# Mixture-of-experts stage of a fused Perceiver kernel: fp32 products replaced by three float32r products of split factors, and work begun one stage earlier

## The chip, the cores and the metric

One core of one Trainium2 chip runs the whole program. The metric is the device time of one execution in microseconds (us); the median of three runs is compared.

## What is computed

Two layers of a Perceiver block on x of shape (2, 256, 256), that is 512 tokens in four tiles of 128 (NT = 4), with a context of 2 x 4096 tokens. Layer 0: cross-attention with 16 heads, low-rank self-attention with 8 heads, and a mixture of 16 experts. Layer 1: cross-attention with top-k and film modulation, retention, and a mixture of adapters. The stage that matters here is the mixture of layer 0, all in fp32:

```
n      = layernorm(x)                       # 512 x 256
probs  = softmax(n @ gate_w.T)              # 16 experts, four kept and rescaled
for e in range(16):                         # every expert is computed for every token
    h  = silu(n @ w1[e]) * (n @ w3[e])      # 512 x 128
    y += weight[:, e] * (h @ w2[e])         # 512 x 256
x      = x + y
```

Between them stands a product of weights alone, the *film products* `Wv @ W_film` (192 x 256 by 256 x 512, twice), which layer 1 reads later.

## The kernel before

The program is written engine by engine, with semaphores (`Flag`): `flag.up(instruction)` counts up when an instruction ends, `engine.wait_ge(*flag.at(n))` waits for a count. Each engine runs its instructions in the order in which they are written; no scheduler moves them. The program is a row of stages. At the end of each, `phase_ends` puts a barrier over all engines, so that a stage begins when the slowest engine is through with the one before. `bank` is the accumulation memory, eight banks of 128 x 512.

**The keys stage**, at the start, already works with split factors: `ch`, `cl` and `w1h`, `w1l` are the high and the low part of a number in float32r, high being the rounded number and low the rest. Its matmuls are L524 (512 columns) and L531 (256 columns).

**The low-rank stage** (`low_*`, L957 to L1131) goes over the four token tiles: `scores(i)` (L1016), the maxima on VectorE (L1101), the exponentials on ScalarE (L1071), `turn` (L1027, transposes), a copy on VectorE (L1109), `weigh` (L1036) and `divide`. Its sync program also fetches `wv1`, `wv2` and `film`. POOL has two small instructions in it.

**The mixture stage** (`moe_*`, L1154 to L1300). TensorE turns `wv1` and `wv2`, then the normalised tokens (L199), then the gate weights (L1179), and makes the gate scores (L1185). VectorE makes the routing weights from them (L1253 to L1274). Then comes a loop over experts. `up(e)` is the pair of products with w1 and w3: four matmuls of 512 columns (L1206) into two banks; two pairs of banks alternate. ScalarE takes Silu of one bank (L1241), VectorE multiplies it with the other (`times_gate`, L1282) into `hid`. `down(e)` is the product with w2: four matmuls of 256 columns (L1217), again with two pairs of banks in turn; VectorE adds them to x with the routing weight (`add`, L1290). TensorE's order is one up ahead:

```
pe.wait_ge(*nm_made.at(1))
up(0)
film_products()
for e in range(NE):
    if e + 1 < NE:
        up(e + 1)
    down(e)
```

Weights lie in four buffers; the sync engine refills one when its down is done. After the stage's barrier the preparation of layer 1 follows (L1373 and on).

## Time and profile before

| | |
|---|---|
| median of 3 runs | 1168.22 us (1164.32 to 1171.87) |
| profiled execution | 1164.9 us, its span 1163.7 us |
| TensorE busy | 969.7 us (83%), 7503 matmuls |
| VectorE, ScalarE busy | 829.5 us (71%), 627.7 us (54%) |
| POOL busy | 258.4 us (22%) |
| granted TensorE clock, mean | 0.889 of 2.4 GHz |
| low-rank stage | about 535 to 594 us of the span |
| mixture stage | about 594 to 702 us of the span |

PE is TensorE's matmul, PEld its weight load, DVE VectorE, ACT ScalarE, SPq the sync engine's DMA queue. A share of busy time is a mean over stages; in the mixture stage TensorE is busy without a break from 606.5 us on, while in the low-rank stage no engine is.

### The profile page before, as it was taken

The numbers are of one execution on the slowest core, as the hardware profiler recorded it, in microseconds if no ns is written. First come the engines' busy times: TensorE is split into PE (matmuls) and PEld (weight loads), VectorE is DVE, ScalarE is ACT, GpSimd is POOL, SyncE is SP. The second block draws the span as 40 slices with busy tenths as digits, with TensorE's granted clock in tenths as the row PEclk, the third lists the DMA queues.
The fourth block names the chain that finished last, engine by engine and source line by source line (L and its number), as shares of the span: only waits on it lengthen the run. The fifth ranks groups of instructions, "written<-read, shape, count | busy, mean of one in ns | idle before, by whom it ended". The sixth has DMA issues, their size and how long they took to land. (4 is left out here: it accounts for less than half of the span.)

```text
span 1163.7 us, 20413 instructions
## 1 busy us (share of the span) xinstructions
PE 969.7 (83%) x7503; PEld 589.6 (51%) x7520; DVE 829.5 (71%) x1753; ACT 627.7 (54%) x1018; POOL 258.4 (22%) x281
## 2 busy tenths in 40 slices
PE   6997769999999999985879998518878878996586
PEld 5886624444444444443765565314455555744354
DVE  5775688999999999913542447998888786256447
ACT  3443317887887888872331114139999998202121
POOL 1000188899300000000000002003554632000010
PEclk9999959999999999997769998558799998997797
DMA  5867632223223223102011216302164226740000
GB/s 179 312 226 256 254 113 73 74 79 83 73 77 86 73 75 86 44 1 57 1 55 62 85 44 181 96 0 60 38 173 133 69 80 213 176 137 1 0 1 19
DMA packets 99319, 111.80 MB, mean 96 GB/s; under 512 B 26658, under 2 KB 75730, under 8 KB 99218
## 3 DMA queue, kind: packets, MB, share of 16 engines
q1 hardware_dynamic: 96802, 109.50, 31.2%
q10 hardware_dynamic: 2416, 0.99, 0.4%
q8 instruction: 60, 0.98, 0.3%
q14 instruction: 41, 0.34, 0.1%
HBM read 80.95 MB, written 29.43 MB: 95 GB/s over the span
## 5 line engine op out<-in xcount | busy, mean ns | idle before, releaser
L835 ACT ACTIVATE pT<-bank 128x512 f32<-128x512 f32 x512 | 278.4, 597 | 93.5 <-PE bank L752 72.2
L857 DVE TENSOR_REDUCE rmax<-bank 128x2 f32<-128x1024 f32 x256 | 307.3, 1223 | 26.5 <-PE bank L720 25.7
L764 PE MATMUL bank<-pT,V 128*17 128x256 f32 x2048 | 161.1, 387 | 4.7 <-ACT oT L841 4.6
L1600 PE MATMUL bank<-K1s,qs 97*128 97x512 f32 x256 | 116.1, 555 | 58.6 <-ACT below L1709 37.2
L752 PEld LDWEIGHTS bank<-qs,ks 49*128 49x128 f32 x1024 | 77.8, 187 | 112.4 <-ACT pT L835 98.9
L752 PE MATMUL bank<-qs,ks 49*128 49x256 f32 x1024 | 130.0, 332 | 2.3 <-ACT pT L835 0.5
L1864 POOL TENSOR_TENSOR total<-total,work 128x1024 f32<-128x1024 f32 x40 | 94.9, 2380 | 154.7 <-ACT work L1718 153.9
L720 PE MATMUL bank<-ks,qs 49*128 49x512 f32 x512 | 110.6, 427 | 16.4 <-DMA ks<-k_parts_d 9.2
L1600 PEld LDWEIGHTS bank<-K1s,qs 97*128 97x128 f32 x256 | 54.0, 224 | 73.9 <-ACT below L1709 38.6
L1770 DVE MAX8 cand<-work 128x8 f32<-128x128 f32 x384 | 76.5, 280 | 0.0
L764 PEld LDWEIGHTS bank<-pT,V 128*17 128x17 f32 x2048 | 34.6, 95 | 63.0 <-ACT pT L835 43.6
L720 PEld LDWEIGHTS bank<-ks,qs 49*128 49x128 f32 x512 | 51.5, 196 | 26.3 <-issue 13.9
L1206 PE MATMUL bank<-xT,w 128*128 128x512 f32 x128 | 60.6, 619 | 0.6 <-DVE nm L1254 0.6
L1634 PE MATMUL bank<-cn,xT 128*128 128x192 f32 x256 | 55.9, 368 | 6.2 <-ACT xT L1728 6.2
L1718 ACT ACTIVATE work<-bank,ebias 128x1024 f32<-128x1024 f32 x48 | 54.9, 1149 | 5.7 <-PE bank L1603 5.4
L1687 ACT COPY work<-bank 128x1024 f32<-128x1024 f32 x48 | 50.8, 1058 | 5.9 <-PE bank L1600 5.9
L1634 PEld LDWEIGHTS bank<-cn,xT 128*128 128x128 f32 x256 | 46.8, 213 | 11.2 <-ACT xT L1728 10.4
L974 POOL MEMSET vA<- 128x32 f32 x1 | 0.2, 154 | 232.4 <-POOLq L113 232.4
L1709 ACT ACTIVATE below<-work,steep_thr 128x2048 bf16<-128x2048 f32 (+1 forms) x26 | 50.2, 1932 | 1.2 <-issue 0.6
L1603 PE MATMUL bank<-below,minus 128*128 128x512 bf16 x111 | 48.2, 434 | 0.0
L1241 ACT ACTIVATE gate<-bank 128x512 f32<-128x512 f32 x16 | 9.6, 597 | 71.0 <-PE bank L1206 71.0
L1282 DVE TENSOR_TENSOR hid<-bank,gate 128x512 f32<-128x512 f32 x16 | 11.1, 692 | 46.2 <-ACT gate L1241 46.2
...
## 6 DMA issues: line engine op xcount, KB each, us to landing
k_parts_d<-kparts SPq DMA_DIRECT2D x48, 512.0 KB, 3.6
...
```

The costliest lines, as they stand in the source:

```text
L720: t = pe.matmul(bank[:, 2 * (at % 2) + a, :], qs[p % 3][rows, qt * P:(qt + 1) * P], ks[p % 2][rows, c * 512:(c + 1) * 512], start=True, st ...
L752: t = pe.matmul(bank[:, 4 + (at + a) % 3, c * S:(c + 1) * S], ks[p % 2][rows, k0:k0 + P], qs[p % 3][rows, :], start=True, stop=True)
L764: t = pe.matmul(bank[32 * c:32 * c + VW, 7, a * S:(a + 1) * S], V[:, b * NCH + 4 * g + c, h, :], pT[:, (at + 2 * (c // 2) + a) % 8, c % 2 ...
L835: p_made.up(act.activation(pT[:, at % 8, :], bank[:, 4 + at % 3, :], ACT.Exp))
L857: max_read.up(dve.tensor_reduce(rmax[p % 2][:, :, qt, c], bank[:, b0:b0 + 2, :], AX.X, ALU.max))
L1206: t = pe.matmul(bank[:, 2 * j + k, :], w13[e % 4][:, k, kt, :], xT[:, kt, :], start=(kt == 0), stop=(kt == 1))
L1600: m = pe.matmul(bank[:, b0 + c, :], qs1[0:NROW1, b * H1 + h, q], K1s[h][0:NROW1, keys], start=True, stop=(what == "new"))
L1634: m = pe.matmul(bank[:, 7, grp % 2 * 256:grp % 2 * 256 + DC], aT[at % 2][:, c, :], cn[at % NCN][:, c, :], start=(n == 0 and c == 0), stop= ...
L1687: s_taken.up(act.copy(home(t)[:, k * 1024:(k + 1) * 1024], bank[:, b0:b0 + 2, :].rearrange("p c n -> p (c n)")))
L1718: s_taken.up(act.activation(home(t)[:, k * 1024:(k + 1) * 1024], bank[:, b0:b0 + 2, :].rearrange("p c n -> p (c n)"), ACT.Exp, bias=ebias[ ...
L1770: m = dve.max(cand[:, g, :], home(t)[:, g * GC:(g + 1) * GC])
L1864: added.up(pool.tensor_tensor(acc[:, part], acc[:, part], home(t)[:, part], ALU.add))
```

## The change

1. In the mixture stage every fp32 factor is split in a high and a low part of type float32r, and a product is the sum of three: high by high, low of the one by high of the other, and the reverse (`PRODUCTS`). The low-by-low product is left out. The split of the tokens (`xTp`) is made once; that of each expert's weights by `expert_high` (ScalarE, rounding copy) and `expert_low` (POOL, subtraction); that of `hid` by `high` (ScalarE) and `low` (VectorE).
2. The ups use three pairs of banks in turn (0 to 5), and run two experts ahead; the downs have one pair (6, 7), and wait bank by bank for the additions of the expert before.
3. The weights of experts 0 to 3 are fetched and split in the low-rank stage. So are `gwr` and `wv` turned there, and the first half of the film products (128 of 192 rows) is made there behind `scores(0)`; the second half (64 rows) is the first work of the mixture stage. VectorE copies the first half, ScalarE the second.
4. `up(0)` waits for the split tokens and no longer for the maxima of the gate scores.

```diff
+    NE, FI, TOP, PAD, WB = 16, 128, 4, 4, 4
...
+    w13p = [sb(f"w13p{j}", [P, 2, 2, 2, FI], F32R) for j in range(WB)]
+    w2p = [sb(f"w2p{j}", [P, 2, D], F32R) for j in range(WB)]
...
+    def load_expert(e):
+        for k, w in enumerate((ins["L0_ffn_w1"], ins["L0_ffn_w3"])):
+            w_in[e % WB].up(sp.dma_start(w13[e % WB][:, k, :, :], w[e].rearrange("(k p) i -> p k i", p=P)), 16)
+        w_in[e % WB].up(sp.dma_start(w2e[e % WB][:, :], ins["L0_ffn_w2"][e]), 16)
+
+    def expert_high(e):
+        j = e % WB
+        act.wait_ge(*w_in[j].at(48 * (e // WB + 1)))
+        wh_split.up(act.copy(w13p[j][:, 0, :, :, :], w13[j][:, :, :, :]))
+        wh_split.up(act.copy(w2p[j][:, 0, :], w2e[j][:, :]))
+
+    def expert_low(e):
+        j = e % WB
+        pool.wait_ge(*wh_split.at(2 * e + 1))
+        wl_split.up(pool.tensor_tensor(w13p[j][:, 1, :, :, :], w13[j][:, :, :, :], w13p[j][:, 0, :, :, :], ALU.subtract))
+        pool.wait_ge(*wh_split.at(2 * e + 2))
+        wl_split.up(pool.tensor_tensor(w2p[j][:, 1, :], w2e[j][:, :], w2p[j][:, 0, :], ALU.subtract))
+
+    FILM_ROWS = (slice(0, P), slice(P, DC))
+
+    def film_products(n, first_bank):
+        pe.wait_ge(*film_w_in.at(32))
+        pe.wait_ge(*wvT_made.at(1))
+        rows = FILM_ROWS[n]
+        for k in range(2):
+            for kt in range(2):
+                t = pe.matmul(bank[0:rows.stop - rows.start, first_bank + k, :], wvT[:, kt, rows], film[:, k, kt, :],
+                              start=(kt == 0), stop=(kt == 1))
+            wvf_made.up(t)
...
+        gate_in.up(sp.dma_start(gwr[:, :], ins["L0_ffn_gate_w"]), 16)
         for k, n in enumerate(("in", "out")):
             film_w_in.up(sp.dma_start(film[:, k, :, :], halves("L1_xattn_W_film_" + n)), 16)
+        for e in range(WB):
+            load_expert(e)
...
         mrow_made.up(pool.tensor_scalar(mrow[:, :], m8[:, :], 1e18, -1e18, ALU.mult, ALU.add))
+        for e in range(WB):
+            expert_low(e)
...
+        pe.wait_ge(*wv_in.at(32))
+        pe.wait_ge(*gate_in.at(16))
+        pe.wait_ge(*qk_made[0].at(1))
+        for kt in range(2):
+            pe.transpose(bank[:, 4, kt * DC:kt * DC + P], wv1[:, kt * P:(kt + 1) * P], ident[:, :])
+            pe.transpose(bank[:, 4, kt * DC + P:(kt + 1) * DC], wv2[:, kt * P:(kt + 1) * P], ident[0:DCM, 0:DCM])
+            t = pe.transpose(bank[:, 4, 2 * DC + kt * NE:2 * DC + (kt + 1) * NE], gwr[:, kt * P:(kt + 1) * P], ident[0:NE, 0:NE])
+        wv_turned.up(t)
         pe.wait_ge(*vA_made.at(NT))
         scores(0)
-        for i in range(NT):
+        film_products(0, 6)
+        for i in range(NT):
+            if i == 0:
+                pe.wait_ge(*wvT_made.at(2))
             turn(2 * i)
+            if i == 0:
+                pe.wait_ge(*wvf_copied.at(2))
             turn(2 * i + 1)
...
+        act.wait_ge(*wv_turned.at(1))
+        wvT_made.up(act.copy(wvT[:, :, :].rearrange("p k c -> p (k c)"), bank[:, 4, 0:2 * DC]))
+        wvT_made.up(act.copy(gwT[:, :, :].rearrange("p a b -> p (a b)"), bank[:, 4, 2 * DC:2 * DC + 2 * NE]))
...
+            expert_high(i)
...
         maxima(0)
+        for k in range(2):
+            dve.wait_ge(*wvf_made.at(k + 1))
+            wvf_copied.up(dve.tensor_copy(wvf1[:, k, :], bank[:, 6 + k, :]))
...
+    xTp = sb("xTp", [P, 2, 2, T], F32R)
...
+    hidp = [sb(f"hidp{j}", [P, 2, T], F32R) for j in range(3)]
+
+    PRODUCTS = ((0, 0), (1, 0), (0, 1))
...
-        for e in range(NE):
-            if e >= 4:
-                sp.wait_ge(*y_made.at(e - 3))
-            for k, w in enumerate((ins["L0_ffn_w1"], ins["L0_ffn_w3"])):
-                w_in[e % 4].up(sp.dma_start(w13[e % 4][:, k, :, :], w[e].rearrange("(k p) i -> p k i", p=P)), 16)
-            w_in[e % 4].up(sp.dma_start(w2e[e % 4][:, :], ins["L0_ffn_w2"][e]), 16)
+        for e in range(WB, NE):
+            sp.wait_ge(*wl_split.at(2 * (e - WB + 1)))
+            sp.wait_ge(*wh_split.at(2 * (e - WB + 1)))
+            load_expert(e)
...
+        film_products(1, 4)
         pe.wait_ge(*ln_made.at(4 * 3))
         turn_tensor(tokens_of(xn))
...
+        def up(e):
+            b0 = 2 * (e % 3)
+            pe.wait_ge(*wh_split.at(2 * e + 1))
+            pe.wait_ge(*wl_split.at(2 * e + 1))
+            if e >= 3:
+                pe.wait_ge(*hid_done.at(e - 2))
+            for k in range(2):
+                for n, (wp, xp) in enumerate(PRODUCTS):
                     for kt in range(2):
-                        t = pe.matmul(bank[0:rows.stop - rows.start, 4 + 2 * n + k, :], wvT[:, kt, rows], film[:, k, kt, :],
-                                      start=(kt == 0), stop=(kt == 1))
-                    wvf_made.up(t)
-
-        def up(e):
-            j = e % 2
-            pe.wait_ge(*w_in[e % 4].at(48 * (e // 4 + 1)))
-            if e >= 2:
-                pe.wait_ge(*hid_done.at(e - 1))
-            for k in range(2):
-                for kt in range(2):
-                    t = pe.matmul(bank[:, 2 * j + k, :], w13[e % 4][:, k, kt, :], xT[:, kt, :], start=(kt == 0), stop=(kt == 1))
+                        t = pe.matmul(bank[:, b0 + k, :], w13p[e % WB][:, wp, k, kt, :], xTp[:, xp, kt, :],
+                                      start=(n == 0 and kt == 0), stop=(n == 2 and kt == 1))
             gu_made.up(t)
 
         def down(e):
-            j = e % 2
-            pe.wait_ge(*hid_done.at(e + 1))
-            if e < 2:
-                pe.wait_ge(*wvf_copied.at(2 * e + 2))
-            else:
-                pe.wait_ge(*y_added.at(NT * (e - 1)))
+            pe.wait_ge(*wh_split.at(2 * e + 2))
+            pe.wait_ge(*wl_split.at(2 * e + 2))
+            pe.wait_ge(*hh_split.at(e + 1))
+            pe.wait_ge(*hl_split.at(e + 1))
             for i in range(NT):
-                t = pe.matmul(bank[:, 4 + 2 * j + i // 2, (i % 2) * D:(i % 2 + 1) * D], hid[j][:, i * P:(i + 1) * P],
-                              w2e[e % 4][:, :], start=True, stop=True)
-            y_made.up(t)
-
+                if i % 2 == 0 and e:
+                    pe.wait_ge(*y_added.at(NT * (e - 1) + i + 2))
+                for n, (hp, wp) in enumerate(PRODUCTS):
+                    t = pe.matmul(bank[:, 6 + i // 2, (i % 2) * D:(i % 2 + 1) * D], hidp[e % 3][:, hp, i * P:(i + 1) * P],
+                                  w2p[e % WB][:, wp, :], start=(n == 0), stop=(n == 2))
+                if i % 2:
+                    y_made.up(t)
+
+        pe.wait_ge(*xh_split.at(2))
+        pe.wait_ge(*xl_split.at(2))
+        up(0)
+        up(1)
+        pe.wait_ge(*wvf_copied.at(4))
         pe.wait_ge(*nm_made.at(1))
-        up(0)
-        film_products()
         for e in range(NE):
-            if e + 1 < NE:
-                up(e + 1)
+            if e + 2 < NE:
+                up(e + 2)
...
+    def moe_pool():
+        for e in range(WB, NE):
+            expert_low(e)
...
+        for k in range(2):
+            act.wait_ge(*wvf_made.at(3 + k))
+            wvf_copied.up(act.copy(wvf2[:, k, :], bank[0:DCM, 4 + k, :]))
+        for kt in range(2):
+            act.wait_ge(*turned.at(2 * 3 + kt + 1))
+            xT_made.up(act.copy(xT[:, kt, :], bank[:, kt, :]))
+            xh_split.up(act.copy(xTp[:, 0, kt, :], bank[:, kt, :]))
...
-        for e in range(NE):
+
+        def silu(e):
             act.wait_ge(*gu_made.at(e + 1))
             if e >= 2:
                 act.wait_ge(*hid_done.at(e - 1))
-            gate_done.up(act.activation(gate[e % 2][:, :], bank[:, 2 * (e % 2), :], ACT.Silu))
-            if e == 0:
-                for n, (dst, rows) in enumerate(((wvf1, P), (wvf2, DCM))):
-                    for k in range(2):
-                        act.wait_ge(*wvf_made.at(2 * n + k + 1))
-                        wvf_copied.up(act.copy(dst[:, k, :], bank[0:rows, 4 + 2 * n + k, :]))
+            gate_done.up(act.activation(gate[e % 2][:, :], bank[:, 2 * (e % 3), :], ACT.Silu))
+
+        def high(e):
+            act.wait_ge(*hid_done.at(e + 1))
+            if e >= 3:
+                act.wait_ge(*y_made.at(2 * (e - 2)))
+            hh_split.up(act.copy(hidp[e % 3][:, 0, :], hid[e % 2][:, :]))
+
+        for e in range(NE + 2):
+            if e < NE:
+                silu(e)
+                high(e)
+            if e >= 2 and e - 2 + WB < NE:
+                act.wait_ge(*gu_made.at(e - 1))
+                act.wait_ge(*y_made.at(2 * (e - 1)))
+                expert_high(e - 2 + WB)
...
+        for kt in range(2):
+            dve.wait_ge(*xh_split.at(kt + 1))
+            xl_split.up(dve.tensor_tensor(xTp[:, 1, kt, :], bank[:, kt, :], xTp[:, 0, kt, :], ALU.subtract))
...
         def times_gate(e):
-            j = e % 2
             dve.wait_ge(*gate_done.at(e + 1))
             if e >= 2:
-                dve.wait_ge(*y_made.at(e - 1))
-            hid_done.up(dve.tensor_tensor(hid[j][:, :], bank[:, 2 * j + 1, :], gate[j][:, :], ALU.mult))
+                dve.wait_ge(*hh_split.at(e - 1))
+            hid_done.up(dve.tensor_tensor(hid[e % 2][:, :], bank[:, 2 * (e % 3) + 1, :], gate[e % 2][:, :], ALU.mult))
+
+        def low(e):
+            dve.wait_ge(*hh_split.at(e + 1))
+            hl_split.up(dve.tensor_tensor(hidp[e % 3][:, 1, :], hid[e % 2][:, :], hidp[e % 3][:, 0, :], ALU.subtract))
 
         def add(e):
-            j = e % 2
-            dve.wait_ge(*y_made.at(e + 1))
             if e:
                 dve.wait_ge(*y_added.at(NT * e))
             for i in range(NT):
-                y_added.up(dve.scalar_tensor_tensor(x[:, i, :], bank[:, 4 + 2 * j + i // 2, (i % 2) * D:(i % 2 + 1) * D],
+                if i % 2 == 0:
+                    dve.wait_ge(*y_made.at(2 * e + i // 2 + 1))
+                y_added.up(dve.scalar_tensor_tensor(x[:, i, :], bank[:, 6 + i // 2, (i % 2) * D:(i % 2 + 1) * D],
                                                     weight[:, i, e:e + 1], x[:, i, :], ALU.mult, ALU.add))
 
-        times_gate(0)
+        for e in range(2):
+            times_gate(e)
+            low(e)
         for e in range(NE):
-            if e + 1 < NE:
-                times_gate(e + 1)
+            if e + 2 < NE:
+                times_gate(e + 2)
             add(e)
+            if e + 2 < NE:
+                low(e + 2)
```

In the low-rank stage, TensorE's order changes as follows (`wv` and `gwr` are the weights that are turned, `sA` the exponentials). Before:

```order
L1004 MATMUL bank<-lowW,xT 128x32 x32
L1016 MATMUL bank<-low_k,low_q 128x256 x8
L1027 MATMUL bank<-ident,sA 128x128 x16
L1016 MATMUL bank<-low_k,low_q 128x256 x8
```

And in the changed kernel:

```order
L1052 MATMUL bank<-lowW,xT 128x32 x32
L1092 MATMUL bank<-ident,wv_8517 128x128
L1093 MATMUL bank<-ident,wv_8518 128x64
L1094 MATMUL bank<-ident,gwr 128x16
L1092 MATMUL bank<-ident,wv_8517 128x128
L1093 MATMUL bank<-ident,wv_8518 128x64
L1094 MATMUL bank<-ident,gwr 128x16
L1064 MATMUL bank<-low_k,low_q 128x256 x8
L977 MATMUL bank<-film,wvT 128x512 x4
L1075 MATMUL bank<-ident,sA 128x128 x16
```

Six transposes stand ahead of scores(0), and four film matmuls between it and the first turn.

On TensorE from the start of the mixture stage (the numbers in the names count buffers). Before:

```order
L199 MATMUL bank<-ident,xn 128x128 x8
L1179 MATMUL bank<-ident,gwr 128x16 x2
L1185 MATMUL bank<-gwT,xT 128x16 x8
L1206 MATMUL bank<-xT,w_0_9036 128x512 x4
L1195 MATMUL bank<-film,wvT 128x512 x4
L1195 MATMUL bank<-film,wvT 64x512 x4
L1206 MATMUL bank<-xT,w_1_9037 128x512 x4
L1217 MATMUL bank<-w2e_9040,hid_9055 128x256 x4
```

And in the changed kernel:

```order
L977 MATMUL bank<-film,wvT 64x512 x4
L199 MATMUL bank<-ident,xn 128x128 x8
L1239 MATMUL bank<-gwT,xT 128x16 x8
L1252 MATMUL bank<-xTp,w13p_8531 128x512 x12
L1252 MATMUL bank<-xTp,w13p_8532 128x512 x12
L1252 MATMUL bank<-xTp,w13p_8533 128x512 x12
L1265 MATMUL bank<-w2p_8535,hidp_9131 128x256 x12
L1252 MATMUL bank<-xTp,w13p_8534 128x512 x12
L1265 MATMUL bank<-w2p_8536,hidp_9132 128x256 x12
```

Three ups stand ahead of the first down where there were two, each of twelve matmuls instead of four. At the other end two downs stand without an up between them, where there were two before as well.

## Rows read from the trace of the kernel before

**Rows 1.** Page, costliest groups: count, then busy us and mean ns, then idle before

```profile
L1206 PE MATMUL bank<-xT,w 128*128 128x512 f32 x128 | 60.6, 619 | 0.6 <-DVE nm L1254 0.6
L1241 ACT ACTIVATE gate<-bank 128x512 f32<-128x512 f32 x16 | 9.6, 597 | 71.0 <-PE bank L1206 71.0
L1282 DVE TENSOR_TENSOR hid<-bank,gate 128x512 f32<-128x512 f32 x16 | 11.1, 692 | 46.2 <-ACT gate L1241 46.2
```

**Rows 2.** Timeline of the mixture stage, in pieces: start us, length us, engine, line

```profile
606.54 6.56 PE L1206 MATMUL bank<-xT,w 128*128 128x512 f32 x8 [0.57 <-DVE nm L1254]
...
612.93 1.45 PE L1195 MATMUL bank<-film,wvT 128*128 128x512 f32 x3
...
620.03 3.70 PE L1206 MATMUL bank<-xT,w 128*128 128x512 f32 x8
...
692.38 3.60 PE L1206 MATMUL bank<-xT,w 128*128 128x512 f32 x8
...
695.81 3.62 PE L1217 MATMUL bank<-w2e,hid 128*128 128x256 f32 x16
...
697.74 3.42 DVE L1290 SCALAR_TENSOR_TENSOR x<-bank,weight,x 128x256 f32<-128x256 f32 x8 [0.41 <-PE bank L1217]
```

**Rows 3.** Windows: length, busy us of PE, PEld, DVE, ACT, POOL, clock, DMA

```profile
594.40:606.50 12.10, 7.30 (x30) 6.06 (x30) 4.15 (x17) 4.42 (x6) 0.00 (x0) 0.50 0.45 131
606.50:613.00 6.50, 6.46 (x9) 2.78 (x10) 3.04 (x32) 2.56 (x9) 0.00 (x0) 0.55 0.00 0
...
620.00:640.00 20.00, 20.00 (x62) 11.61 (x62) 7.17 (x16) 2.97 (x5) 0.00 (x0) 1.00 0.28 90
```

**Rows 4.** Timeline of the keys stage, one block's float32r matmuls, first and last

```profile
60.11 0.39 PE L524 MATMUL bank<-ch,w1h 128*128 128x512 f32 x1
...
62.17 0.40 PE L524 MATMUL bank<-c,w2l 128*128 128x512 f32 x1
62.41 0.28 PE L531 MATMUL bank<-w1h,ch 128*128 128x256 f32 x1
...
64.58 0.28 PE L531 MATMUL bank<-w2l,c 128*128 128x256 f32 x1
```

**Rows 5.** Windows, the same stretch of the keys stage

```profile
60.00:64.80 4.80, 4.80 (x32) 4.20 (x30) 3.94 (x6) 2.18 (x4) 0.00 (x0) 1.00 0.41 155
```

**Rows 6.** Groups kept apart by shape, VectorE and POOL: busy us, mean ns

```profile
L443 DVE TENSOR_TENSOR qparts<-qf,qparts 128x512 fp32r<-128x512 f32 x2 | 1.4, 692 | 0.1
...
L1864 POOL TENSOR_TENSOR total<-total,work 128x1024 f32<-128x1024 f32 x40 | 94.9, 2380 | 154.7 <-ACT work L1718 153.9
...
L602 POOL TENSOR_TENSOR fr<-g,g 128x128 f32<-128x128 f32 x9 | 4.1, 456 | 0.7
```

**Rows 7.** Timeline of the low-rank stage up to the first copy of turned scores

```profile
541.91 0.47 SPq L969 DMA_DIRECT2D film<-in_L_xattn_W_film_out  x1
...
552.85 1.15 PE L1016 MATMUL bank<-low_k,low_q 32*128 32x256 f32 x16 [1.87 <-DVE vA L1093]
...
556.39 3.03 ACT L1071 ACTIVATE sA<-bank,mA 128x256 f32<-128x256 f32 x8 [5.26 <-DVE mA L1101]
...
558.01 3.46 PE L1027 MATMUL bank<-ident,sA 128*128 128x128 f32 x16 [4.01 <-ACT sA L1071]
...
560.02 1.23 DVE L1109 COPY sAT<-bank 128x1024 f32<-128x1024 f32 x1 [3.66 <-PE bank L1027]
```

**Rows 8.** DMA issues: count, KB each, median us from issue to landing

```profile
film<-in_L_xattn_W_film_out SPq DMA_DIRECT2D x1, 512.0 KB, 7.1
```

**Rows 9.** Timeline of the seam before the first up

```profile
599.66 1.97 PE L199 MATMUL bank<-ident,xn 128*128 128x128 f32 x8 [3.71 <-DVE xn L184]
...
602.40 3.57 PE L1185 MATMUL bank<-gwT,xT 128*128 128x16 f32 x16 [0.45 <-ACT xT L205]
...
610.54 0.65 DVE L1274 TENSOR_SCALAR weight<-weight,den 128x16 f32<-128x16 f32 x4
```

More of the change, by code:

```diff
@@ L932, in build @@
     wvf_d = nc.dram_tensor("wvf_d", [DC, 2, 2 * D], F32).ap()
+    NE, FI, TOP, PAD, WB = 16, 128, 4, 4, 4
+    w13 = [sb(f"w13_{i}", [P, 2, 2, FI]) for i in range(WB)]
+    w2e = [sb(f"w2e_{i}", [P, D]) for i in range(WB)]
+    w13p = [sb(f"w13p{j}", [P, 2, 2, 2, FI], F32R) for j in range(WB)]
+    w2p = [sb(f"w2p{j}", [P, 2, D], F32R) for j in range(WB)]
+    gwr = sb("gwr", [NE, D])
+    gwT = sb("gwT", [P, 2, NE])
+    w_in = [flag(f"w_in{i}") for i in range(WB)]
+    gate_in, wh_split, wl_split = flag("gate_in"), flag("wh_split"), flag("wl_split")
@@ L933, in build @@
     mask_d = nc.dram_tensor("mask_d", [NB, S2], F32).ap()
     mask_in, mrow_made, mask_stored = flag("mask_in"), flag("mrow_made"), flag("mask_stored")
-    film_w_in, wv_turned, wvT_made, wvf_made, wvf_copied, wvf_stored = (flag(n) for n in (
-        "film_w_in", "wv_turned", "wvT_made", "wvf_made", "wvf_copied", "wvf_stored"))
+    wv_in, film_w_in, wv_turned, wvT_made, wvf_made, wvf_copied, wvf_stored = (flag(n) for n in (
+        "wv_in", "film_w_in", "wv_turned", "wvT_made", "wvf_made", "wvf_copied", "wvf_stored"))
@@ L1132, in build @@
     phase_ends()
-    NE, FI, TOP, PAD = 16, 128, 4, 4
     phase_begins()
-    w13 = [sb(f"w13_{i}", [P, 2, 2, FI]) for i in range(4)]
-    w2e = [sb(f"w2e_{i}", [P, D]) for i in range(4)]
-    gwr = sb("gwr", [NE, D])
-    gwT = sb("gwT", [P, 2, NE])
     lg = sb("lg", [P, NT, NE])
@@ L1169, in moe_tensor @@
     def moe_tensor():
-        pe.wait_ge(*film_w_in.at(64))
-        for kt in range(2):
-            pe.transpose(bank[:, 4, kt * DC:kt * DC + P], wv1[:, kt * P:(kt + 1) * P], ident[:, :])
-            t = pe.transpose(bank[:, 4, kt * DC + P:(kt + 1) * DC], wv2[:, kt * P:(kt + 1) * P], ident[0:DCM, 0:DCM])
-        wv_turned.up(t)
+        film_products(1, 4)
         pe.wait_ge(*ln_made.at(4 * 3))
         turn_tensor(tokens_of(xn))
-        pe.wait_ge(*gate_in.at(16))
-        for kt in range(2):
-            t = pe.transpose(bank[:, 2, kt * NE:(kt + 1) * NE], gwr[:, kt * P:(kt + 1) * P], ident[0:NE, 0:NE])
-        gw_turned.up(t)
-        pe.wait_ge(*gwT_made.at(1))
         pe.wait_ge(*xT_made.at(8))
@@ L1184, in moe_tensor @@
             for kt in range(2):
-                t = pe.matmul(bank[:, 3, i * NE:(i + 1) * NE], xT[:, kt, i * P:(i + 1) * P], gwT[:, kt, :],
+                t = pe.matmul(bank[:, 7, i * NE:(i + 1) * NE], xT[:, kt, i * P:(i + 1) * P], gwT[:, kt, :],
                               start=(kt == 0), stop=(kt == 1))
         lg_made.up(t)
-        def film_products():
-            pe.wait_ge(*wvT_made.at(1))
-            for rows, n in ((slice(0, P), 0), (slice(P, DC), 1)):
-                for k in range(2):
-                    for kt in range(2):
-                        t = pe.matmul(bank[0:rows.stop - rows.start, 4 + 2 * n + k, :], wvT[:, kt, rows], film[:, k, kt, :],
-                                      start=(kt == 0), stop=(kt == 1))
-                    wvf_made.up(t)
@@ L1231, in moe_scalar @@
-        wvT_made.up(act.copy(wvT[:, :, :].rearrange("p k c -> p (k c)"), bank[:, 4, 0:2 * DC]))
         norm_scalar(2)
-        turn_scalar(3)
+        for k in range(2):
[5 more added lines that the diff above has]
+            xh_split.up(act.copy(xTp[:, 0, kt, :], bank[:, kt, :]))
```

21 lines of the change are left out of this document (7 added, 14 removed).

## The prediction, made before the changed kernel ran

> **What bounds the kernel now.** I read the page first (which engines are busy in which stretch), then the costliest groups, then the mixture stage in order of time, then the two neighbours that receive moved work. The chain of waits at the end of the page covers only the last few per cent of the span, so it says nothing on this stage; who waits for whom there must be read from the groups and the timeline.
>
> In the mixture stage TensorE never waits: its first products (L1206) sat idle 0.6 us in all before 128 instructions, while ScalarE waited 71.0 us for them and VectorE 46.2 us for ScalarE [rows 1]. The timeline shows the period. The first up(0) starts at 606.54; the film products start at 612.93; up(1) at 620.03, and up(15) at 692.38, so 14 pairs of one up and one down take 72.35 us, **5.17 us a pair** [rows 2]. Then come up(15) (3.43), two downs (3.62) and VectorE's last additions until 701.16. Adding up: 6.39 + 7.10 + 72.35 + 3.43 + 3.62 + 1.73 = **94.6 us** from 606.54 to 701.16. The windows say at what clock: 0.50 in the part before 606.5, 0.55 until 613, 1.00 after it, with TensorE busy 20.00 of 20.00 us [rows 3]. So up(0) paid 6.39 us for the work that later costs 3.43.
>
> **The price of a split product.** The kernel already multiplies float32r factors in its keys stage, in both forms that the change uses: 128 weights by 512 columns (L524) and by 256 columns (L531). Starts are to be compared there, not durations, since matmuls overlap. From 60.11 to 62.17 lie 9 starts: 0.229 us each; from 62.41 to 64.58 lie 19: 0.114 us each [rows 4], at a granted clock of 1.00 [rows 5]. An fp32 matmul is two instructions in the trace (x8 for four in the program), a float32r one is one. Hence an up becomes 12 x 0.229 = 2.75 us (was 3.43), a down 12 x 0.114 = 1.37 us (was 1.73): **4.12 us a pair**, three products included. The nearest other row is the fp32 matmul itself, 3.43 / 4 = 0.857 us, four times 0.214 [rows 2]. If a float32r matmul were exactly a quarter of it, the pair would cost 3.9; I take 4.12 because rows 4 are the very form.
>
> The Trainium skill (TensorE: Matmul & The Clock Gate, "Back-to-back issue gap") gives N / 2.4 + 2.5 ns warm, 216 ns for 512 columns and 109 ns for 256. By it the pair would be 3.90 us and the stage some 4 us shorter still; the rows of the keys stage do not agree with it, being 6% above.
>
> **Does another engine become the bound?** Per expert, VectorE has its product with the gate (0.69), a new subtraction (0.69, as L443 [rows 6]) and four additions (3.42 / 8 = 0.43 each [rows 2], 1.71): 3.1 of 4.12 us. ScalarE has Silu of 512 elements (0.60 [rows 1]) and three casts of 512 or fewer, taken at the same price: at most 2.4. POOL has two subtractions of 512 and 256 elements; between 0.456 us for 128 and 2.38 for 1024 [rows 6] lies a line that gives 1.28 + 0.73 = 2.0. The waits fit too. Counted from the end of up(e+2): Silu, gate product and additions of e are done after about 3.2 us, and down(e+1), which needs the one pair of result banks, comes after 4.1. ScalarE's cast of hid ends at 2.2, its cast of the next weights at 2.8, POOL's subtraction at 4.1, and up(e+4), which reads them, starts at 1.37 + 2.75 + 1.37 = 5.5. So 0.9 and 1.4 us are left, and TensorE stays the bound. The next weights are asked for four pairs ahead, 16 us, so their transfers stay hidden.
>
> **The sum for the stage.** up(0) to up(15) is 16 x 2.75 = 44.0, down(0) to down(13) beside them 14 x 1.37 = 19.2. Then the single pair of result banks shows: down(14) and down(15) must wait, bank by bank, for the additions before them. VectorE does add(13) 1.7, the last subtraction 0.7, add(14) 1.7, then down(15)'s second half 0.7 + 0.2, then the last two additions 0.9, with hand-overs of some 0.2: 6.1 us (before: downs 3.62 and additions 1.73 after the last up, for two downs). Together 44.0 + 19.2 + 6.1 = **69.3 us against 94.6: 25.3 less**. Some 7.1 of it are the film products, which leave this stretch; 16 instructions, eight to each side.
>
> **Film products, first half, and the transposes, in the low-rank stage.** The six transposes fall between the value products and scores(0), which waits until 552.85 for VectorE, 1.9 us of idle TensorE: hidden. The four matmuls follow scores(0), end of it at 554.0, and the next TensorE work is turn(0) at 558.01 [rows 7]. At the high clock they need 7.10 / 2 = 3.55 us [rows 2]: done at 557.6, before turn(0). At the low clock they need 8 x 0.80 = 6.4 (up(0), rows 2): done at 560.4, 2.4 us late. TensorE was at work shortly before and now does not idle, so I take zero and keep +2.4; on the other side, turn(0) and turn(1) may run at the higher clock, at most 1.5 us of 3.46. The last film weights are issued at 541.91 [rows 7] and take 7.1 us to land [rows 8]: there at 549, or 549.5 behind one more small issue, in time. The two VectorE copies (0.6 to 0.7 each, half of the 1.23 for 1024 elements) stand between the maxima (end 556.4) and the first copy of turned scores at 560.02 [rows 7]: hidden; with the film products late they would end with them, inside the same 2.4 us. The casts of experts 0 to 3 take about 1 us after each tile's exponentials, where ScalarE waits for the next tile's maxima (5.3 us before the first [rows 7]), and POOL had nothing. Twelve DMA issues move ahead of the mask's store on SP's queue; only the next stage needs that store.
>
> **Film products, second half, at the seam.** They need 3.6 us at the high and 6.4 at the low clock from 594.5, in place of 1.4 us of transposes. xn comes at 599.66 as before [rows 9]. At the low clock the turn starts at 600.9, and ScalarE's two copies and then four instead of two transfers of xT (0.59 each) put the gate scores, now at 602.40, up to 2 us later; on the other side TensorE has then worked without a break before the turn, and turn (1.97) and gate scores (3.57 [rows 9]) may run at the high clock. The first up no longer waits for the maxima. I put its start between 604.1 and 607.5 and take **605.5, 1.0 earlier**, and charge half of a low-clock up(0), 1.4 us. VectorE's routing ends 5.2 us after the gate scores, as now (606.0 to 611.2 [rows 9]); down(0) comes 8.2 us after them, behind three ups: hidden, which it was not to the same degree when one up stood there.
>
> **Sum:** -25.3 - 1.0 + 1.4 + 0 = -24.9 us. The profiled execution took 1164.9 us, so 1140.0. The median of the runs is 3.3 above it (1168.2); the changed kernel's median should lie at **1142 us**.
>
> **Rivals.**
> 1. *VectorE and POOL get in each other's way.* The new subtraction on VectorE reads two SBUF tiles, and POOL now works in this stage. No row of this kernel shows such a pair overlapping, so I bound it: nothing, or each subtraction waits for one POOL instruction, 3.1 + 1.28 = 4.4 us a pair, +0.28 x 16 = 4.5; at the outermost for both, 5.1, +15. It gives 1147 to 1157. Against it: POOL idles half of each pair, and VectorE 1 us. The Trainium skill (SBUF — State Buffer, "Who interferes with whom") says that a VectorE instruction with two SBUF inputs and a GpSimd instruction that reads SBUF exclude each other for their whole length. No run here shows it yet; by it this rival is real, and the first bound holds. Chance 0.13.
> 2. *The array takes 3.9 us a pair,* a quarter of the fp32 time for each product: 1138. Chance 0.08.
> 3. *POOL is the bound.* No POOL row writes float32r. From twice the price above (2.0 to 4.1) it sets the pace; at 2.6 times the pair is 5.2 us, as before, and only the film products and the early start are gained, some 8 us: 1160, within the noise. Chance 0.04.
> 4. *Slower: the granted clock stays at 1.2 GHz in the mixture.* Each pair would cost 4.12 more; 24.9 / 4.12 = 6, so from the seventh such pair the kernel is slower than before, and with all 16 it ends at 1208. For it: the seam, with TensorE busy 7.30 of 12.10 us, is at 0.50 [rows 3]. Against it: float32r products in the keys stage are at 1.00 [rows 5], and nothing here leaves TensorE idle. Chance 0.03.
>
> The forecast itself has 0.72. The range takes in the lower rate and the better seam below (1168.2 - 25.3 - 2.4 - 1.5 - 4 = 1135, and 3 us of spread), and above the first port bound with the low-clock film products (1142 + 4.5 + 2.4 and spread): 1132 to 1153. A difference under 1% (11.7 us) can't be told from none here: faster 0.93, same 0.04, slower 0.03.
>
> **What the new profile would show.** Starts of consecutive ups 4.1 us apart with TensorE without a gap; float32r matmuls 0.229 us apart; VectorE's new subtraction at 0.69 us (longer: rival 1); POOL's two at 1.28 and 0.73 (longer: rival 3); clock 1.00 from the first or second up on; turn(0) of the low-rank stage still about 3.9 us after scores(0) ends. I am wrong if an up waits for POOL's weights or a down for additions in mid-stage, or if the low-rank stage grows by more than 3 us.

## The result, and the profile after

| | before | after |
|---|---|---|
| median, same chip | 1170.05 us (4 runs) | **1141.89 us** (1139.02 to 1143.56, 4 runs) |
| profiled execution, its span | 1164.9, 1163.7 us | 1140.79, 1139.5 us |
| low-rank stage | 59.3 us | 56.1 us |
| seam, to the first up | 12.0 us | 9.5 us |
| mixture, first up to last addition | 94.6 us | 72.1 us |
| next stage, to its first product with K1s | 14.6 us | 17.9 us |

The ratio is 0.9766, 95% interval 0.9734 to 0.9798: faster, and the forecast of 1142.0 was met. The medians differ by 28.2 us, the two profiled executions by 24.1. In a second comparison both kernels ran again unchanged (runs r1 and r2, below), and their medians differ by 25.5 us.

The costliest groups of the changed kernel in the window 590 to 673 us, the mixture stage; they answer to [rows 1] and, for the new instructions, to [rows 6]. Columns: shapes and count, busy us and mean ns, idle us before them and what ended it.

```profile
L1252 PE MATMUL bank<-xTp,w13p 128*128 128x512 f32 x192 | 48.7, 406 | 0.0
...
L1265 PE MATMUL bank<-w2p,hidp 128*128 128x256 f32 x192 | 25.3, 280 | 1.4 <-DVE x L1365 1.4
...
L1357 DVE TENSOR_TENSOR hidp<-hid,hidp 128x512 fp32r<-128x512 f32 x16 | 22.0, 1377 | 1.4 <-ACT hidp L1308 1.4
L963 POOL TENSOR_TENSOR w13p<-w,w13p 128x512 fp32r<-128x512 f32 x12 | 15.5, 1291 | 45.4 <-ACT w13p L957 45.4
L965 POOL TENSOR_TENSOR w2p<-w2e,w2p 128x256 fp32r<-128x256 f32 x12 | 14.4, 1196 | 0.0
L1353 DVE TENSOR_TENSOR hid<-bank,gate 128x512 f32<-128x512 f32 x16 | 11.1, 693 | 7.9 <-ACT gate L1302 7.8
```

TensorE still waits for nothing: 0.0 us before 192 up products, 1.4 before the down products, all of it in the tail. But two of the new instructions are longer than forecast: VectorE's subtraction took 1377 ns where 690 was expected (1.61 us in the twelve experts in which POOL works beside it, 0.69 in the other four), POOL's second one 1196 where 730 was. The gate product is unchanged at 693.

The timeline has one whole pair (start us, length us, engine, line, and the idle time before where there was any), then the last up and the tail. It answers to [rows 2].

```profile
600.38 4.13 PE L1252 MATMUL bank<-xTp,w13p 128*128 128x512 f32 x11
...
610.41 1.57 PE L1265 MATMUL bank<-w2p,hidp 128*128 128x256 f32 x12
...
611.82 2.97 PE L1252 MATMUL bank<-xTp,w13p 128*128 128x512 f32 x12
...
616.04 2.97 PE L1252 MATMUL bank<-xTp,w13p 128*128 128x512 f32 x12
616.07 1.65 DVE L1365 SCALAR_TENSOR_TENSOR x<-bank,weight,x 128x256 f32<-128x256 f32 x4
616.18 0.62 ACT L1308 CAST hidp<-hid 128x512 fp32r<-128x512 f32 x1 [0.76 <-DVE hid L1353]
...
616.71 0.62 ACT L957 CAST w13p<-w 128x512 fp32r<-128x512 f32 x1
...
617.40 1.29 POOL L963 TENSOR_TENSOR w13p<-w,w13p 128x512 fp32r<-128x512 f32 x1 [1.76 <-ACT w13p L957]
617.63 1.60 DVE L1357 TENSOR_TENSOR hidp<-hid,hidp 128x512 fp32r<-128x512 f32 x1
...
618.65 1.19 POOL L965 TENSOR_TENSOR w2p<-w2e,w2p 128x256 fp32r<-128x256 f32 x1
...
662.38 2.96 PE L1252 MATMUL bank<-xTp,w13p 128*128 128x512 f32 x12
...
667.64 1.67 PE L1265 MATMUL bank<-w2p,hidp 128*128 128x256 f32 x12 [0.88 <-DVE x L1365]
...
669.80 1.67 PE L1265 MATMUL bank<-w2p,hidp 128*128 128x256 f32 x12 [0.50 <-DVE x L1365]
...
670.86 1.66 DVE L1365 SCALAR_TENSOR_TENSOR x<-bank,weight,x 128x256 f32<-128x256 f32 x4 [0.42 <-PE bank L1265]
```

From up(3) at 611.82 to up(15) at 662.38 lie 12 pairs: **4.213 us each**, where 5.17 stood and 4.12 was forecast. An up takes 2.81 us from its start to that of the down (12 starts, 0.234 each), a down 1.41 (0.1175 each). VectorE's subtraction begins 0.23 us after POOL's and ends at 619.23, 0.54 after POOL's end at 618.69: it does its own work when POOL is through. POOL's second one in turn ends at 619.84, 0.61 after VectorE. The only waits of TensorE are in the tail, for the additions.

Windows of the same trace (length, busy us of PE, PEld, DVE, ACT, POOL, granted clock, DMA), answering to [rows 3]:

```profile
602.00:604.00 2.00, 2.00 (x6) 1.51 (x6) 1.36 (x18) 1.64 (x4) 0.00 (x0) 0.50 0.00 1
604.00:606.00 2.00, 2.00 (x9) 1.58 (x8) 1.90 (x16) 0.60 (x1) 0.00 (x0) 0.78 0.00 0
...
620.00:640.00 20.00, 20.00 (x113) 17.26 (x112) 18.28 (x30) 9.64 (x19) 11.30 (x10) 1.00 0.34 100
```

The clock is at its low level for a part of the first ups, and at the high one from then on, as before. VectorE is now busy 18.28 of 20 us; some of that is standing still behind POOL.

### The profile page after: what moved, and what is told of

Its sections match the earlier page's. It is cut to its first block and busy times, and to the rows that moved or that the text cites. A ratio compares the mean times of both kernels' runs of the same rounds, so it can differ in the third digit from the quotient of the medians.

```text
span 1139.5 us, 20829 instructions
## 1 busy us (share of the span) xinstructions
PE 955.4 (84%) x7631; PEld 599.1 (53%) x7648; DVE 848.7 (74%) x1772; ACT 651.4 (57%) x1067; POOL 295.7 (26%) x313
## 5 line engine op out<-in xcount | busy, mean ns | idle before, releaser
L1713 PE MATMUL bank<-cn,xT 128*128 128x192 f32 x256 | 59.1, 383 | 6.3 <-ACT xT L1807 6.2
L1713 PEld LDWEIGHTS bank<-cn,xT 128*128 128x128 f32 x256 | 49.4, 222 | 11.5 <-ACT xT L1807 10.5
L1252 PE MATMUL bank<-xTp,w13p 128*128 128x512 f32 x192 | 48.7, 406 | 0.0
L963 POOL TENSOR_TENSOR w13p<-w,w13p 128x512 fp32r<-128x512 f32 x16 | 20.6, 1286 | 80.8 <-ACT w13p L957 80.8
L1252 PEld LDWEIGHTS bank<-xTp,w13p 128*128 128x128 f32 x192 | 36.2, 194 | 7.9
```

What stands on the lines that cost most here:

```text
L1252: t = pe.matmul(bank[:, b0 + k, :], w13p[e % WB][:, wp, k, kt, :], xTp[:, xp, kt, :], start=(n == 0 and kt == 0), stop=(n == 2 and kt == 1))
L1713: m = pe.matmul(bank[:, 7, grp % 2 * 256:grp % 2 * 256 + DC], aT[at % 2][:, c, :], cn[at % NCN][:, c, :], start=(n == 0 and c == 0), stop= ...
```

## The experiments

Stage lengths are from each kernel's profile. They are sharper than the medians: the mixture took 72.1 us in the changed kernel's two profiles and in e2's, which shares its code there, while the executions of one kernel spread over 4 to 14 us. Against the kernel before, the intervals of e2, e3, e5, e6 and e8 all overlap that of the changed kernel, so their medians alone part none of them from it.

### What the product is worth: e1

```diff
-    w13p = [sb(f"w13p{j}", [P, 2, 2, 2, FI], F32R) for j in range(WB)]
+    w13p = [sb(f"w13p{j}", [P, 2, 2, 2, FI], F32) for j in range(WB)]
...
-    PRODUCTS = ((0, 0), (1, 0), (0, 1))
+    PRODUCTS = ((0, 0),)
```

w2p, xTp and hidp become fp32 too, so that one fp32 product does the work of the three.

> The changed kernel with all its moves (film products, early weights, order two experts ahead, casts and their buffers) but fp32 products: one matmul per factor pair instead of three, and the copies keep fp32. Theory A (the gain of the mixture is the cheaper product): a pair of up and down costs 5.16 us again instead of 4.21, so the stage is 14 x 0.95 = 13 to 15 us longer and the kernel comes to about 1156 us; half of the 28 us of gain stays, from the moved work. Rival (the gain is order and moves, the product's price does not matter): within 3 us of 1142.

Measured: 1156.97 us, ratio 0.9897 (0.9828 to 0.9966). The mixture took 86.7 us, the seam 9.5. Two consecutive ups in the timeline:

```profile
631.02 3.60 PE L1252 MATMUL bank<-xTp,w13p 128*128 128x512 f32 x8
...
636.18 2.31 PE L1252 MATMUL bank<-xTp,w13p 128*128 128x512 f32 x5
```

They start 5.16 us apart, the price of fp32. So of the 22.5 us by which the mixture became shorter, 14.6 (86.7 to 72.1) are the price of the product and 7.9 (94.6 to 86.7) the moves, above all the film products' 7.1 [rows 2]; with the seam's 2.5 the moves are worth 10.4.

### The film products: e2

```diff
         scores(0)
-        film_products(0, 6)
...
     def moe_tensor():
+        film_products(0, 2)
         film_products(1, 4)
```

Their copies go to ScalarE in the mixture stage, and up(1) waits for them.

> The changed kernel with the first half of the film products back in the mixture stage, before the second half, on banks 2 and 3; its copies go to ScalarE. Theory A (behind scores(0) the film matmuls were free, and beyond that kept the granted clock up, which made the low-rank stage 3.2 us shorter): the low-rank stage goes back to 59 us (+3), the seam before the first up grows by the 3.5 to 6.9 us of eight instructions less what waits for the tokens anyway, some +4; about 1149 us. Rival (the low-rank stage's 3.2 us are chance of that execution): the stage stays at 56 us, about 1146.

Measured: 1147.09 us, ratio 0.9780 (0.9699 to 0.9860); one of its four executions took 4566.31 us, which no trace explains, and the other three lie at 1140.66 to 1147.74. The seam grew from 9.5 to 13.3 us, and the film products there are one group:

```profile
595.21 9.10 PE L977 MATMUL bank<-film,wvT 128*128 128x512 f32 x16 [1.48 <-PEq L113]
```

The mixture stayed at 72.1. The early half is thus worth 3.8 us of seam. What failed is the thought that these products, filling TensorE's idle time, keep the clock high and so shorten the low-rank stage: without them it took 55.8 us, as short as with them.

### Does POOL reach the bound, and what does the exclusion cost: e3, e5

e3 doubles each subtraction of POOL from expert 4 on; e5 cuts them to 4 columns (most of the low parts of those weights are left out).

```diff
+        if e >= WB:
+            gps.then(pool.tensor_tensor(w13p[j][:, 1, :, :, :], w13[j][:, :, :, :], w13p[j][:, 0, :, :, :], ALU.subtract))
         wl_split.up(pool.tensor_tensor(w13p[j][:, 1, :, :, :], w13[j][:, :, :, :], w13p[j][:, 0, :, :, :], ALU.subtract))
```

```diff
-        wl_split.up(pool.tensor_tensor(w13p[j][:, 1, :, :, :], w13[j][:, :, :, :], w13p[j][:, 0, :, :, :], ALU.subtract))
+        m = 1 if e >= WB else FI
+        wl_split.up(pool.tensor_tensor(w13p[j][:, 1, :, :, 0:m], w13[j][:, :, :, 0:m], w13p[j][:, 0, :, :, 0:m], ALU.subtract))
```

> The changed kernel with each of POOL's two subtractions done twice for experts 4 to 15. Theory A (VectorE's subtraction of two SBUF tiles and POOL's instructions shut each other out for their whole length): POOL needs 2 x (1.29 + 0.73) = 4.0 us a pair and cannot start while VectorE's 0.69 runs, nor the reverse, so POOL and VectorE together set the pace: pair 4.7 to 5.4 us instead of 4.21, kernel +6 to +14 us. Rival (they share without shutting out; the 1.60 us of VectorE's subtraction is something else): POOL's 4.0 stays below 4.21, pair unchanged, kernel within 1 us of 1142.

> The changed kernel with POOL's subtraction cut to a few columns for experts 4 to 15, so that their low parts are mostly those of experts 0 to 3 (left out on purpose). Theory A (exclusion, but hidden): VectorE's subtraction falls from 1.60 to 0.69 us, the pair stays 4.21 us, kernel within 1 us of 1142. Rival 1 (VectorE's 1.60 us is its own price for float32r output from SBUF): it stays 1.60. Rival 2 (the exclusion does cost time): the pair falls towards 4.12.

e3 measured 1147.61 us, ratio 0.9808 (0.9740 to 0.9876): the mixture took 76.7 us, 4.6 more, at 4.6 us a pair. In its groups POOL idles for 26.0 us in all, and all of it lies before its first instruction in this stage:

```profile
L964 POOL TENSOR_TENSOR w13p<-w,w13p 128x512 fp32r<-128x512 f32 x12 | 20.5, 1708 | 26.0 <-ACT w13p L957 26.0
L965 POOL TENSOR_TENSOR w13p<-w,w13p 128x512 fp32r<-128x512 f32 x12 | 15.9, 1326 | 0.9
L1361 DVE TENSOR_TENSOR hidp<-hid,hidp 128x512 fp32r<-128x512 f32 x14 | 10.5, 752 | 0.0
...
L968 POOL TENSOR_TENSOR w2p<-w2e,w2p 128x256 fp32r<-128x256 f32 x12 | 8.9, 743 | 0.0
L969 POOL TENSOR_TENSOR w2p<-w2e,w2p 128x256 fp32r<-128x256 f32 x12 | 8.9, 742 | 0.9
```

1.71 + 1.33 + 0.74 + 0.74 = 4.52 us of POOL in a pair of 4.6: POOL has become the bound. Here VectorE's subtraction comes first and is short (0.68 to 0.72 us in all but the first such pair, where it took 1.61), and it is POOL's that is long. The timeline of e3:

```profile
630.06 0.68 DVE L1361 TENSOR_TENSOR hidp<-hid,hidp 128x512 fp32r<-128x512 f32 x1
630.15 1.74 POOL L964 TENSOR_TENSOR w13p<-w,w13p 128x512 fp32r<-128x512 f32 x1
```

So it goes both ways.

e5 measured 1143.68 us, ratio 0.9780 (0.9719 to 0.9842), the mixture 72.2 us at 4.21 a pair, no shorter than with whole subtractions. Its timeline shows two POOL instructions of one size beside and clear of VectorE:

```profile
635.87 0.21 POOL L964 TENSOR_TENSOR w13p<-w,w13p 128x4 fp32r<-128x4 f32 x1 [3.25 <-ACT w13p L957]
636.10 0.68 DVE L1359 TENSOR_TENSOR hidp<-hid,hidp 128x512 fp32r<-128x512 f32 x1
636.18 0.66 POOL L967 TENSOR_TENSOR w2p<-w2e,w2p 128x4 fp32r<-128x4 f32 x1
```

Four columns take POOL 0.21 us alone; 0.08 us behind the start of VectorE's subtraction they take 0.66 and end with it or just after. The subtraction itself is back at 0.68. **The two engines exclude each other, and here it costs nothing**, since no up and no down waits for either: in the pair shown above VectorE's subtraction for down(3) ends at 619.23, and down(3) starts at 623.05, one pair after down(2); POOL's for up(5) ends at 618.69, and up(5) starts at 620.25.

### How far ahead the ups run: e6

```diff
         up(0)
-        up(1)
...
-            if e + 2 < NE:
-                up(e + 2)
+            if e + 1 < NE:
+                up(e + 1)
             down(e)
```

VectorE's order is changed to match.

> The changed kernel with ups one expert ahead instead of two, VectorE's order to match. Theory A (exclusion of VectorE and POOL, hidden by the second expert ahead): down(e) now waits for VectorE's subtraction, which ends only after POOL's, pair 4.6 us, stage +7 us, about 1149. Rival (no exclusion matters): VectorE's subtraction is done 3.9 us after the up, just inside the 4.2, pair 4.22, and only the first and last experts cost 2 us more, about 1144.

Measured: 1147.38 us, ratio 0.9803 (0.9746 to 0.9859); the mixture took 77.9 us, 5.8 more. (Its later stages were also 9 us longer in the profiled execution, which I can't explain; the stage length is the better figure.) The timeline shows the wait:

```profile
632.95 2.97 PE L1252 MATMUL bank<-xTp,w13p 128*128 128x512 f32 x12
...
634.44 1.61 DVE L1356 TENSOR_TENSOR hidp<-hid,hidp 128x512 fp32r<-128x512 f32 x1
...
636.31 1.65 PE L1265 MATMUL bank<-w2p,hidp 128*128 128x256 f32 x12 [0.39 <-DVE hidp L1356]
```

TensorE idles until VectorE's subtraction ends at 636.05, and that one stood behind POOL (1.61 us). At 0.69 us it would have ended at 635.13, before the up beside it was through (635.92); so the wait is put down to the exclusion by this sum, and no run has one up ahead without the exclusion. One up between up(e) and down(e) is too little cover; a second one hides both the chain and the exclusion. Pairs alternate between about 4.3 and 4.9 us.

### Another narrow type: e4 and its repeat r3

```diff
-    w13p = [sb(f"w13p{j}", [P, 2, 2, 2, FI], F32R) for j in range(WB)]
+    w13p = [sb(f"w13p{j}", [P, 2, 2, 2, FI], BF16) for j in range(WB)]
```

w2p, xTp and hidp likewise; the three products are kept. How much exactness it costs is not on record.

> The changed kernel with factors split into two bf16 parts instead of two float32r parts; 24 products a pair as before. Theory A (the 0.234 us between starts is a property of 4-byte factors): starts come 0.216 us apart or less, pair 3.9 us, and with the exclusion of VectorE and POOL perhaps 4.0; stage -3 to -5 us, about 1138. Rival (the spacing comes from the weight loads that alternate with the matmuls, whatever the type): 0.234 stays, pair 4.2, about 1142. Its products are less exact than those of float32r.

> The kernel with bf16 parts once more, beside the changed kernel on the same chip. Theory A (matmuls of 2-byte factors start 0.216 us apart against 0.234): mixture 67.4 against 72.1 us, median 4 to 5 us below the changed kernel's. Rival (the earlier 3.6 us between their medians were chance): within 2 us.

Measured: 1138.33 us, ratio 0.9729 (0.9681 to 0.9777); the repeat 1138.16, ratio 0.9734 (0.9697 to 0.9771). The timeline of e4:

```profile
633.07 2.75 PE L1252 MATMUL bank<-xTp,w13p 128*128 128x512 bf16 x12
635.66 1.47 PE L1265 MATMUL bank<-w2p,hidp 128*128 128x256 bf16 x12
636.97 2.75 PE L1252 MATMUL bank<-xTp,w13p 128*128 128x512 bf16 x12
```

and its group of weight loads, at 98 ns each (the changed kernel's same group, for float32r, has 188):

```profile
L1265 PEld LDWEIGHTS bank<-w2p,hidp 128*128 128x128 bf16 x185 | 17.9, 98 | 7.3 <-issue 2.1 <-DVE x L1365 0.2
```

2.59 us for 12 starts is 0.216 each, 1.31 is 0.109: 3.90 us a pair, the second rival's number, but for bf16. Both the matmuls and their weight loads are shorter with bf16, and no run tells which of the two lowers the spacing. The mixture took 67.4 and 65.5 us; the clock under its first ups stood at 0.50 to 0.67 in the one and at 1.00 in the other. It is the best version in median, 4.3 us below r2. The two intervals overlap slightly, and the stage length is what shows it.

### The stages around it: e7, e8, and both kernels again

e7 is the kernel before with four fp32 matmuls of 512 columns behind scores(0), where the change has its film products; e8 is the changed kernel with two such at the end of each of the first three tiles of the low-rank stage. Their results are read by nobody.

```diff
         scores(0)
+        for k in range(2):
+            for kt in range(2):
+                pe.matmul(bank[:, 6 + k, :], ident[:, :], ones[:, :], start=(kt == 0), stop=(kt == 1))
```

```diff
             weigh(2 * i + 1)
+            for k in range(2 if i + 1 < NT else 0):
+                pe.matmul(bank[:, 5, :], ident[:, :], ones[:, :], start=(k == 0), stop=(k == 1))
```

> The kernel before with nothing changed but four fp32 matmuls of 512 columns, whose result nobody reads, behind scores(0), where the changed kernel has its film products. Theory A (filling TensorE there keeps the granted clock up): the low-rank stage falls from 59.3 to about 56 us although work is added, kernel -3 us. Rival (the film products only moved into idle time): the stage stays at 59.3 us, kernel unchanged or slower.

> The changed kernel with two more fp32 matmuls of 512 columns, whose result nobody reads, at the end of each of the first three tiles of the low-rank stage, where TensorE waits for the exponentials. Theory A (idle stretches there let the clock fall, and each tile at the low clock takes 9.8 instead of 7.8 to 8.3 us): tiles 2 and 3 fall to about 8 us, low-rank stage -2 to -3 us, about 1139. Rival (filling one gap does not hold the clock through the small products of the weigh step): tiles as now or the fill is in the way, 1142 to 1144.

> The kernel before, unchanged, profiled once more. Theory A (the low-rank and the preparation stage have several lengths for one and the same program, by where in them the granted clock falls and rises): low-rank stage 59.3 or some 56 us, preparation up to the first scores 14.6 or 17.6 to 19 us. Rival (the low-rank stage is 59.3 us in this program and 56 in the changed one): 59.3 again. Mixture from its first up to its last addition 94.7 us either way.

> The changed kernel, unchanged, profiled once more. Theory A: mixture 72.1 us and seam 9.5 us again, low-rank stage 56.1 or 59.2, preparation 14.6 or 17.9; median about 1142. Rival (the preparation is 3 us longer in the changed kernel): 17.9 again.

| us | run | ratio (interval) | low-rank | seam | mixture | next stage's start |
|---|---|---|---|---|---|---|
| e7 | 1169.46 | 1.0010 (0.9985 to 1.0034) | 59.2 | 12.0 | 94.7 | 17.7 |
| e8 | 1147.31 | 0.9820 (0.9773 to 0.9867) | 58.2 | 10.2 | 70.6 | 14.6 |
| r1, before | 1167.97 | 0.9997 (0.9973 to 1.0022) | 59.4 | 12.0 | 94.7 | 14.6 |
| r2, after | 1142.43 | 0.9786 (0.9745 to 0.9826) | **59.0** | 9.9 | 72.1 | **14.6** |
| after, first profile | 1141.89 | 0.9766 (0.9734 to 0.9798) | **56.1** | 9.5 | 72.1 | **17.9** |

The last two lines are one program. Its low-rank stage lasted 56.1 us in one execution and 59.0 in the other, and the start of the next stage 17.9 and 14.6: both differences are the granted clock's. In the low-rank stage, the first profile of the changed kernel, the windows where the film products L977 run:

```profile
552.80:554.80 2.00, 2.00 (x17) 0.94 (x13) 1.28 (x1) 0.79 (x1) 0.00 (x0) 1.00 0.02 4
554.80:556.80 2.00, 2.00 (x6) 0.74 (x4) 1.61 (x2) 0.95 (x3) 0.00 (x0) 1.00 0.00 0
```

its timeline:

```profile
553.38 3.70 PE L977 MATMUL bank<-film,wvT 128*128 128x512 f32 x8
...
557.56 1.06 PE L1075 MATMUL bank<-ident,sA 128*128 128x128 f32 x8 [0.48 <-ACT sA L1135]
```

and the same windows and timeline of r2:

```profile
553.50:555.50 2.00, 2.00 (x16) 0.88 (x11) 1.28 (x1) 0.79 (x1) 0.00 (x0) 0.72 0.01 1
555.50:557.50 2.00, 2.00 (x4) 0.75 (x3) 1.02 (x1) 0.95 (x3) 0.00 (x0) 0.50 0.00 0
```

```profile
554.09 5.40 PE L977 MATMUL bank<-film,wvT 128*128 128x512 f32 x8
559.32 2.04 PE L1075 MATMUL bank<-ident,sA 128*128 128x128 f32 x16
```

With the clock falling to the low level under them, the film products take 5.40 us instead of 3.70, and turn(0) starts 5.2 us after the end of scores(0) instead of 4.1 (4.0 in the kernel before). At the start of the next stage it is the first execution that has the low level. The clock, in windows, and its 16 projections, in the timeline:

```profile
681.00:683.00 2.00, 1.23 (x5) 0.67 (x4) 0.00 (x0) 1.73 (x3) 0.00 (x0) 0.50 0.71 223
683.00:685.00 2.00, 2.00 (x3) 0.57 (x2) 1.56 (x5) 0.23 (x2) 0.00 (x0) 0.50 0.51 161
```

```profile
682.44 9.24 PE L1498 MATMUL bank<-xT,wq 128*96 128x512 f32 x16 [0.77 <-ACT xT L205]
```

In r2 the clock was 1.00 there, and the same row reads:

```profile
685.33 7.08 PE L1498 MATMUL bank<-xT,wq 128*96 128x512 f32 x16 [0.82 <-ACT xT L205]
```

The other profiles of the changed program fall into the same two groups. Where the film products took 3.70 us (the changed kernel's first profile, e1, e3, e4, e6), the low-rank stage lasted 56.1 to 56.2 us; where they took 5.40 (r2, r3, e5), 59.0 to 59.2. The kernel before took 59.3 and 59.4, and e2, without film products there, 55.8. Of nine profiles of the changed program and its variants (e8 left out) six have the short stage, of three of the program before (e7 with them) none. Whether another part of the change makes the short case more frequent, these few profiles don't show.

Filling the idle time did not help: e7 kept a low-rank stage of 59.2 us, and e8 had 58.2 and no better median; in both, the eight instructions behind scores(0) took 5.40 us as well. (e8's shorter mixture is the clock of the first ups again: 1.00, and three ups in 8.5 us.) Whatever decides in which phase the clock stands when a stage with idle time begins, these runs don't show it; that stays open.

## Why the prediction was right, step by step

| step | predicted | measured | shown by |
|---|---|---|---|
| pair, up and down | 4.12 us | 4.213 us | starts, after |
| first three ups | 8.25 + 1.4 | 10.03 | 600.38 to 610.41 |
| from up(15) to the end | 10.2 (2.75 + 1.37 + 6.1) | 10.14 | 662.38 to 672.52 |
| mixture | 69.3 us | 72.1 us | |
| seam | -1.0 (+1.4) | -2.5 | 12.0 to 9.5 |
| mixture and seam | **-24.9** | **-25.0** | e1 parts it |
| low-rank stage | 0 (-1.5 to +2.4) | -3.2, in r2 -0.2 | r2 |
| next stage | not spoken of | +3.3, in r2 0 | r2 |

**The price of the product held.** The keys stage [rows 4] gave 0.229 and 0.114 us a start, the mixture shows 0.234 and 0.1175: 0.09 us a pair, 1.1 us over 12 pairs. The Trainium skill's 216 and 109 ns (TensorE: Matmul & The Clock Gate, "Back-to-back issue gap") are what bf16 shows here (e4), and not what float32r does. Reading the price at the same form in another stage was right; the skill's figure would have given a pair 0.3 us too short. Why the same form starts 2% further apart in the mixture than in the keys stage is not shown.

**The first ups were slower than allowed, the seam shorter.** Three ups took 10.03 us, 1.8 above three at full speed where 1.4 were charged; in e8, at clock 1.00, they took 8.5. The seam gave back 1.5 more than forecast: film products 5.32 us, turn 1.09 where [rows 9] has 1.97, gate scores 1.96 where they have 3.57.

```profile
591.02 5.32 PE L977 MATMUL bank<-film,wvT 128*64 128x512 f32 x8 [1.48 <-PEq L113]
...
596.27 1.09 PE L199 MATMUL bank<-ident,xn 128*128 128x128 f32 x8
...
598.58 1.96 PE L1239 MATMUL bank<-gwT,xT 128*128 128x16 f32 x16 [1.22 <-ACT xT L1292]
```

The range had this outcome (turn and gate scores at the high clock), the forecast did not. So the mixture's 72.1 is 69.3 with 1.1 for the pairs and 1.8 for the first ups, of which 1.4 stood in the sum elsewhere; the 1.4 that is left over and the seam's 1.5 cancelled. That the sum came out to 0.1 us is luck; its parts were right to about 1.5.

**The median was met by luck as well.** The prediction adds 3.3 us to 1140.0 and writes 1142; the sum is 1143.3, and the 1.3 us have no reason. The profiled execution took 1140.79, so the stages' sum held to 0.8, helped by the 3.2 and 3.3 us of the two neighbouring stages, which it did not foresee and which cancelled. The median of the kernel before had risen from 1168.22 to 1170.05 in the comparison, and the difference was 28.2 us where 24.9 stood. In the second comparison it was 25.5, near the 25.0 that the two stages account for; the rest of the 28.2 has no cause that a trace shows.

**The waits came as worked out.** POOL's subtraction was to be ready 1.4 us before its up, and is 1.56 (618.69 to 620.25) before it; the additions 0.9 before their down, and are 1.1 (617.72 to 618.84). VectorE's longer subtraction delays neither.

**Rival 1 was a true mechanism with a wrong price.** The chance of 0.13 was for a pair lengthened by 0.28 us or more. VectorE's subtraction grew from 0.69 to 1.60 us and POOL's from 0.73 to 1.19, as the Trainium skill has it (SBUF — State Buffer, "Who interferes with whom"): of two such instructions the second waits until the first is through. The trace agrees but for a small overlap: VectorE's subtraction ends 0.54 us after POOL's, and takes 0.69 alone. e5 took the exclusion away and the pair stayed at 4.21. The step that failed in it is the bound "3.1 + 1.28": VectorE's subtraction does not wait for a whole POOL instruction but for what is left of one that began 0.23 us before it, 0.9 us, so VectorE is busy 18.28 of 20 us, 3.85 in a pair of 4.21, and still not the bound. e6 shows what the distance between subtraction and reader is for. **Rival 3** (POOL as the bound): its two instructions take 2.5 us of the pair, so 1.7 are left; doubled, they make the pair 0.4 longer (e3). **Rival 2** (a quarter of the fp32 time) is true of bf16 alone. **Rival 4** (low clock throughout) did not occur; the clock was 1.00 from 606 us on.

**The low-rank stage was predicted unchanged, and no lasting change is shown.** One profile shows it 3.2 us shorter and the next stage's start 3.3 longer, the other neither. Had only the first been read, the film products would have been credited with a gain; e2 (without them, 55.8) and r2 (with them, 59.0) show that the short stage does not need them, and that they do not ensure it. They cost nothing at either clock: the first tile, from maxima to maxima, took 8.4 us where they took 5.40 (r2) and 7.7 where they took 3.70, against 8.5 in e2 and 8.6 in the kernel before. The prediction had turn(0) 2.4 us late at the low clock; in r2, where the clock stood at 0.72 and then 0.50, it was 1.2 late, and the tile absorbed it.

What was not tried is the mixture with POOL's and VectorE's subtractions kept apart in time by their order; after e5 there is nothing for it to win in this pair, though with bf16 products, where VectorE is busy 19.04 of 20 us (r3, 620 to 640), there might be.
